# Graph attention on one core: half of M from scaled fp16 parts, joined probabilities, and a new order in the first rounds

## The reference

```python
h = relu((x - mean) / sqrt(var + 1e-05))
output = einsum('bni,io->bno', h, weight)
q, k = einsum('bni,io->bno', h, wq), einsum('bni,io->bno', h, wk)
alpha = einsum('bno,bmo->bnm', q, k)
alpha = maximum(alpha, 0.0) * (adj != 0)
alpha = softmax(alpha, axis=1)
return x + einsum('bnm,bmo->bno', alpha, output)
```

## Time and profile before

| | us |
|---|---|
| median of 3 runs | 412.75 (412.72 to 412.98) |
| the profiled execution | 412.91 |
| its span | 411.1 |
| TensorE busy | 405.3 (99%) |
| VectorE busy | 298.1 (73%) |
| ScalarE busy | 277.7 (68%) |
| GpSimd busy | 264.7 (64%) |

### The profile page before, as it was taken

One profiled execution on the slowest core, in us unless ns is written; L12 is line 12 of the kernel. 1 busy time (PEld: TensorE's weight loads), 2 busy tenths in 40 slices (PEclk: granted clock), 3 DMA queues, 4 the chain that ended last, 5 costly groups with the idle time before them and its releaser, 6 DMA issues.

```text
span 411.1 us, 9529 instructions
## 1 busy us (share of the span) xinstructions
PE 405.3 (99%) x3580; PEld 321.7 (78%) x3580; DVE 298.1 (73%) x571; ACT 277.7 (68%) x592; POOL 264.7 (64%) x286
## 2 busy tenths in 40 slices
PE   8999999999999999999999999999999999999995
PEld 5444545979797997979798897979889797979884
DVE  5797789896867676776767777676777667656565
ACT  4749887765867677766777776776867777644534
POOL 0767896979495866759395775939577584910004
PEclk9999999999999999999999999999999999999999
DMA  8973858989889897997969498985978599493022
GB/s 284 373 110 67 217 103 217 232 205 217 181 208 191 245 155 212 189 204 188 192 212 196 156 214 199 197 218 173 198 241 158 156 220 181 75 197 112 2 104 102
DMA packets 161641, 75.03 MB, mean 183 GB/s; under 512 B 135360, under 2 KB 143808, under 8 KB 161600
## 3 DMA queue, kind: packets, MB, share of 16 engines
q1 hardware_dynamic: 161168, 73.81, 77.6%
q10 hardware_dynamic: 432, 0.66, 0.4%
HBM read 24.12 MB, written 16.78 MB: 99 GB/s over the span
## 4 chain that ended last, share of the span: by engine, by line
PE 90%; DVE 4%; DMA 2%; ACT 1%; SPq 1%; issue 1%; POOL 0%; DVEq 0%; POOLq 0%
PE bank L1166 10%; PE bank L1165 10%; PE bank L1163 10%; PE bank L1181 10%; PE bank L1180 10%; PE bank L1178 10%; PE s_bank L1192 3%; PE s_bank L1193 3%; PE s_bank L1194 3%; PE bank L1199 2%; PE bank L1200 2%; PE bank L1201 2%; PE bank L1320 2%; PE bank L1322 2%; PE bank L1321 2%; DMA x_sb<-in_x 2%
## 5 line engine op out<-in xcount | busy, mean ns | idle before, releaser
L423 POOL TENSOR_TENSOR hn_lo<-h,hn_hi 128x512 f16<-128x512 f32 x64 | 74.0, 1166 | 53.1 <-ACT hn_hi L554 52.9
L544 ACT ACTIVATE h<-x_sb,shift,rstd 128x512 f32<-128x512 f32 x64 | 50.0, 804 | 24.0 <-POOL shift L418 23.6
L449 POOL TENSOR_TENSOR hn_lo<-s,hn_hi 128x512 f16<-128x512 f32 x56 | 63.3, 1163 | 0.3 <-ACT hn_hi L559 0.3
L1163 PE MATMUL bank<-hT_hi,mt_hi 128*128 128x256 f16 x224 | 61.1, 273 | 0.0
L1165 PE MATMUL bank<-hT_lo,mt_hi 128*128 128x256 f16 x224 | 61.1, 273 | 0.0
L1180 PE MATMUL bank<-wt_lo,hT_hi 128*128 128x256 f16 x224 | 61.1, 273 | 0.0
L1166 PE MATMUL bank<-hT_hi,mt_lo 128*128 128x256 f16 x224 | 61.1, 273 | 0.0
L1178 PE MATMUL bank<-wt_hi,hT_hi 128*128 128x256 f16 x224 | 61.1, 273 | 0.0
L1181 PE MATMUL bank<-wt_hi,hT_lo 128*128 128x256 f16 x224 | 61.1, 273 | 0.0
L559 ACT ACTIVATE hn_hi<-s 128x512 f16<-128x512 f32 x56 | 33.8, 625 | 25.6 <-POOL s L438 19.9
L1180 PE MATMUL bank<-w_lo,hT_hi 128*128 128x256 f16 x168 | 45.8, 273 | 0.0
(11 more groups left out here) (169 smaller groups left out, 1115.2 us busy)
## 6 DMA issues: line engine op xcount, KB each, us to landing
out_h<-x_sb SPq DMA_DIRECT2D x63, 256.0 KB, 2.1
x_sb<-in_x SPq DMA_DIRECT2D x15, 1024.0 KB, 5.5
adj_sb<-in_adj SPq DMA_DIRECT2D x16, 256.0 KB, 5.3
hn_hi<-in_L_gnn_wq SPq DMA_DIRECT2D x4, 256.0 KB, 5.6
x_sb<-in_x SPq DMA_DIRECT2D x2, 512.0 KB, 7.2
w_sb<-in_L_gnn_weight SPq DMA_DIRECT2D x2, 512.0 KB, 8.7
hn_lo<-in_L_gnn_wk ACTq DMA_DIRECT2D x2, 256.0 KB, 3.8
hn_lo<-in_L_gnn_wk SPq DMA_DIRECT2D x2, 256.0 KB, 3.7
```

Source lines behind the costliest of these rows:

```text
L423: nc.gpsimd.tensor_tensor(hn_lo[:, s, b], h[:, b], hn_hi[:, s, b], ALU.subtract).then_inc(h_split, 1)
L449: nc.gpsimd.tensor_tensor(low, s32[:, f], high, ALU.subtract).then_inc(s_split, 1)
L544: nc.scalar.activation(h[:, b], x_sb[:, s, b], ACT.Relu, bias=shift[:, b:b + 1], scale=rstd[:, b:b + 1]).then_inc(h_made, 1)
L1163: nc.tensor.matmul(o, bh[:, k, cols], ah[:, :, k], start=first and c == 0 and k == 0, stop=False, skip_group_check=True)
```

## The change

- **M.** Chunks 2 and 3 (`PARTS`) are made of fp16 parts. ScalarE makes high parts of wk and of two rows of wq, and a scaled copy of three quarters of wk. GpSimd makes three low parts of wk, VectorE the fourth and the low parts of wq. TensorE makes 24 products of 512 columns in place of 8 exact ones.
- **Scales.** wk, wq and W have a chain each (`top`, `top_row`, `power`; `spread_top`, `spread_row` on TensorE).
- **First V.** Its products go part by part, with a semaphore for each transpose.
- **Probabilities.** VectorE scales the exponentials in place, 128x512 at once; ScalarE makes the high part in one activation, VectorE the low part in one operation.
- **SP, round 1.** The transpose of the lows of group 2's sums moves behind the stores of group 0 and the load of x of group 4.
- **GpSimd.** The scales of group 3 come ahead of the last low of group 2's sums, those of group 4 behind the first low of group 3's.
- **VectorE and ScalarE, rounds 0 to 2.** A new order: in round 2 the mask of group 3 and the fourth `mt_lo` come behind the residuals, ahead of `sum_c22_t`; the exponentials and high parts of group 0 come two activations earlier.

```diff
@@ SP @@
+            def transpose_sums_hi(g):
                 sp.wait_ge(s_hi_made, sums(g, 4))
                 transpose_part(hT_hi, hn_hi, g % 2, GB, sT_landed)
+            def transpose_sums_lo(g):
                 sp.wait_ge(s_split, sums(g, 4))
                 transpose_part(hT_lo, hn_lo, g % 2, GB, sT_landed)
...
                     transpose_h(g + 1)
-                    transpose_sums(g + 1)
+                    transpose_sums_hi(g + 1)
+                    if g > 1:
+                        transpose_sums_lo(g + 1)
                 store(g - 1)
                 if g + 3 < G:
                     sp.wait_ge(stored[(g - 1) % UNROLL], 16 * GB * ((g - 1) // UNROLL + 1))
                     load_x(g + 3)
+                if g == 1:
+                    transpose_sums_lo(2)
                 if g + 1 < G:
                     transpose_mask(g + 1)
@@ GpSimd @@
-            lows_of_sums(2, 0)
-            layernorm_scales(3)
+            lows_of_sums(2, 0, scales=3, scales_at=3)
             sums_of_h(3, 1)
-            lows_of_sums(3, 1)
+            lows_of_sums(3, 1, scales=FIRST + 2, scales_at=1)
@@ ScalarE @@
+            act.wait_ge(scale_step, KEY_SCALED)
+            act.wait_ge(wkT_copied, K)
+            for k in range(K):
+                if k < 3:
+                    nc.scalar.activation(wk_scaled[:, k], wkT[:, k].rearrange("p r n -> p (r n)"), ACT.Copy,
+                                         scale=key_scale).then_inc(wk_scaled_made, 1)
+                nc.scalar.activation(wk_hi[:, k], wkT[:, k].rearrange("p r n -> p (r n)"), ACT.Copy,
+                                     scale=key_scale).then_inc(wk_hi_made, 1)
...
-                for b in graphs:
-                    nc.scalar.activation(p_hi[:, b], exps[:, b], ACT.Copy, scale=row_inv[:, b:b + 1]).then_inc(p_hi_made, 1)
+                nc.scalar.activation(p_hi[:], exps[:], ACT.Copy).then_inc(p_hi_made, GB)
@@ VectorE @@
+            def probabilities(g):
+                vec.wait_ge(inv_made, g + 1)
+                nc.vector.tensor_tensor(exps[:], exps[:], row_inv[:].unsqueeze(2).to_broadcast([N, GB, N]),
+                                        ALU.mult).then_inc(p_made, 1)
             def lo_of_p(g):
-                for b in range(GB):
-                    vec.wait_ge(p_hi_made, GB * g + b + 1)
-                    nc.vector.scalar_tensor_tensor(p_lo[:, b], exps[:, b], row_inv[:, b:b + 1], p_hi[:, b], ALU.mult,
-                                                   ALU.subtract).then_inc(p_split, 1)
+                vec.wait_ge(p_hi_made, GB * g + GB)
+                nc.vector.tensor_tensor(p_lo[:], exps[:], p_hi[:], ALU.subtract).then_inc(p_split, GB)
...
                 for b in range(1, GB):
                     residual(g - 1, (j - 1) % UNROLL, b)
+                if isinstance(g, int) and g == FIRST:
+                    lo_of_mt(3)
+                    make_mask(3, 1, 2)
+                    vec.wait_ge(mt_split, 4)
                 sum_c22_t(g)
...
+            vec.wait_ge(w_maxed, K)
+            top(KEY)
+            query_max(0)
+            top_row(KEY, 0)
+            query_max(1)
+            power(KEY, 0, 0)
+            query_max(2)
+            query_max(3)
+            vec.wait_ge(w_maxed, 2 * K)
+            top(QUERY)
+            stats_first(0)
+            stats_first(1)
+            top_row(QUERY, 1)
+            power(QUERY, 1, KEY_SCALED)
+            stats_first(2)
+            stats_first(3)
@@ TensorE @@
-            product_m(2, range(1))
-            pe.wait_ge(top_step, 3)
-            pe.wait_ge(consts_made, 5)
-            nc.tensor.matmul(top_bank[:, N:N + 3], ones[:], top_diag[:], start=True, stop=True).then_inc(top_filled, 1)
-            product_m(2, range(1, K))
-            product_m(3)
+            pe.wait_ge(wk_hi_made, K)
+            for c in PARTS:
+                pe.wait_ge(wq_hi_made, c - PARTS[0] + 1)
+                for k in range(K):
+                    scaled_m(c, wq_hi, wk_hi, k, start=k == 0)
+            spread_top(W, 2)
+            pe.wait_ge(wk_lo_pool, 3)
+            for c in PARTS:
+                for k in range(3):
+                    scaled_m(c, wq_hi, wk_lo, k)
+            spread_row(W, 2)
+            for c in PARTS:
+                pe.wait_ge(wq_lo_made, c - PARTS[0] + 1)
+                for k in range(K):
+                    scaled_m(c, wq_lo, wk_hi, k)
+            pe.wait_ge(wk_lo_vec, 1)
+            for c in PARTS:
+                scaled_m(c, wq_hi, wk_lo, 3, stop=True)
```

More of the change, by code:

```diff
@@ L157, in graph_attention_kernel @@
         shift = sb("shift", [N, GB], F32)
+        W, QUERY, KEY = range(3)
+        w_scale, key_scale, query_scale = (scale_of[:, i:i + 1] for i in (W, KEY, QUERY))
+        m_factor = W_TOP / (4 * D)
+        M_BACK = m_factor / 2.0 ** (2 * W_SHIFT)
         row_max = sb("row_max", [N, GB], F32)
@@ L253, in graph_attention_kernel @@
         s_split = sem("s_split")
-        hT0_landed = [sem(f"hT0_landed{b}") for b in range(3)]
+        hT0_hi_landed = [sem(f"hT0_hi_landed{b}") for b in range(3)]
+        hT0_lo_landed = [sem(f"hT0_lo_landed{b}") for b in range(3)]
         hT_landed = [sem(f"hT_landed{s}") for s in range(2)]
@@ L1006, in _, with top @@
             nc.vector.memset(alpha[:, 0:2], 0.0).then_inc(alpha_zeroed, 1)
[L1007 to L1014 removed]
+            def top(i):
+                nc.vector.tensor_reduce(w_top[:, i:i + 1], w_max[:, i], AX.X, ALU.max).then_inc(top_step, 1)
@@ L1031, in _ @@
-            vec.wait_ge(scale_step, 2)
-            nc.vector.tensor_scalar(w_scale[:].bitcast(I32), pow2[:, 0:1].bitcast(I32), -1.0, INV_BITS + W_SHIFT * 2.0 ** 23,
-                                    ALU.mult, ALU.add).then_inc(scale_step, 1)
+            top(W)
+            lo_of_wq(PARTS[0])
+            top_row(W, 2)
+            for r in PARTS[1:]:
+                lo_of_wq(r)
+            power(W, 2, M_SCALED + 1)
+            lo_of_wk(3)
             for k in range(K):
                 vec.wait_ge(w_hi_made, k + 1)
-                nc.vector.scalar_tensor_tensor(w_lo[:, k], w_sb[:, k], w_scale[:], w_hi[:, k], ALU.mult,
+                nc.vector.scalar_tensor_tensor(w_lo[:, k], w_sb[:, k], w_scale, w_hi[:, k], ALU.mult,
@@ L1053, in _ @@
+            stats_all(1, 1, 0)
+            stats_all(1, 1, 1)
             for k in range(K):
                 vec.wait_ge(m_hi_made, k + 1)
-                nc.vector.scalar_tensor_tensor(m_lo[:, k], M_BANK[k], m_scale[:], m_hi[:, k], ALU.mult,
+                nc.vector.scalar_tensor_tensor(m_lo[:, k], M_BANK[k], m_scale[:] if k not in PARTS else M_BACK, m_hi[:, k], ALU.mult,
                                                ALU.subtract).then_inc(m_split, 1)
+            stats_all(1, 1, 2)
+            stats_all(1, 1, 3)
@@ L1074, in _ @@
             softmax_sum(0)
+            probabilities(0)
             lo_of_p(0)
@@ L1103, in _ @@
             softmax_sum(LAST - 1)
+            probabilities(LAST - 1)
             lo_of_p(LAST - 1)
@@ L1303, in product_m, with spread_top, spread_row, scaled_m @@
                     last.then_inc(m_filled, 1)
+            def spread_top(i, n):
+                pe.wait_ge(top_step, 2 * n + 1)
+                nc.tensor.transpose(top_bank[0:1, 0:N], w_top[:, i:i + 1], ident[:]).then_inc(top_filled, 1)
+            def spread_row(i, n):
+                pe.wait_ge(top_step, 2 * n + 2)
+                pe.wait_ge(consts_made, 5)
+                nc.tensor.matmul(top_bank[:, N:N + 1], ones[:], top_col[:, i:i + 1], start=True, stop=True).then_inc(top_filled, 1)
+            def scaled_m(c, left, right, k, start=False, stop=False):
+                mm = nc.tensor.matmul(M_BANK[c], left[:, c - 2, k], right[:, k], start=start, stop=stop)
+                if stop:
+                    mm.then_inc(m_filled, 1)
+            def first_v(b, left, right, k, start=False, stop=False):
+                mm = nc.tensor.matmul(v_bank(0)[b], left[:, 0, b, k], right[:, k], start=start, stop=stop)
+                if stop:
+                    mm.then_inc(whole_v, 1)
             def whole_product_v(g, b):
@@ new lines, in _ @@
+            pe.wait_ge(wk_lo_vec, 1)
+            for c in PARTS:
+                scaled_m(c, wq_hi, wk_lo, 3, stop=True)
+            pe.wait_ge(hT0_hi_landed[0], 16)
+            for k in range(K):
+                pe.wait_ge(w_hi_made, k + 1)
+                first_v(0, hT_hi, w_hi, k, start=k == 0)
+            pe.wait_ge(hT0_lo_landed[0], 16)
+            for k in range(K):
+                first_v(0, hT_lo, w_hi, k)
+            pe.wait_ge(hT0_hi_landed[1], 16)
+            for k in range(K):
+                first_v(1, hT_hi, w_hi, k, start=k == 0)
@@ new lines, in _ @@
+            for k in range(K):
+                pe.wait_ge(w_split, k + 1)
+                first_v(0, hT_hi, w_lo, k, stop=k == K - 1)
+            for k in range(K):
+                first_v(1, hT_hi, w_lo, k)
+            pe.wait_ge(hT0_lo_landed[1], 16)
+            for k in range(K):
```

(9 more changed lines are left out.)

325 lines of the change are left out of this document (192 added, 133 removed).

## The result

The changed kernel takes 413.43 us (median of 21 runs, 413.0 to 414.32), the kernel before 412.73 in the same series (412.58 to 413.67, 21 runs). The ratio is 1.0016, 95% interval 1.0010 to 1.0023: 0.7 us slower, within the 0.2% that the prediction called no change, and resolved from zero only because there are so many runs. The profiled execution took 413.73, its span 411.9, 0.8 more than before.

The account below looks back on a forecast made before the run. TensorE, busy throughout from 97.10 to 380.00, was taken as the bound, so only time before 97.10 counted. Terms -0.8 - 0.2 + 0.8 + 0.2 = 0.0 against 412.91 gave 412.9; 8-in-10 range 411.6 to 414.1, with 0.1 above.

Parts of the forecast that it names:

- both terms of round 2: Round 2: TensorE's wait for the lows behind x, +0.8, and its wait for sum_c22_t on VectorE, +0.2.
- The start: Up to t's first product: fewer products for M let t start at 30.9 instead of 31.73, -0.8.
- rival B: Start gives nothing: m_scale and s_unscale at 1.24 each beside GpSimd delay W's top; 414.1, slower; chance 0.12.
- The outputs of group 0: Joined probabilities and earlier ScalarE activations close TensorE's 0.19 hole ahead of these outputs, -0.2.
- The lows behind x: Round 2: lows' transposes queued behind x of group 4 are ready at 74.7, wanted by TensorE at 73.9, +0.8.
- Rival A: Both round 2 waits stay away, the lows landing 0.6 behind x like the mask; 411.9, down to 411.6; chance 0.22.
- The landing beside the end of x: Alternative reading of the skill's section: lows counted as landed at 72.8, making their round 2 term 0.
- mt_lo and the mask: Round 2 on VectorE: both stand behind the residuals, ahead of sum_c22_t, ready 90.6 against TensorE's arrival at 90.4, +0.2.
- Nothing from round 3 on: Rounds from 3 on and the tail: no hole on TensorE, no term.
- What costs nothing: Joined probabilities from round 3 on, GpSimd's reordered scales, earlier x loads and ScalarE's ten activations for M: no cost.
- Rival C: Lows come late: x issued 3.85 after the last residual, a wait of 2.0 rather than 0.8; 413.9 left; chance 0.13.

Follow-up runs that it names:

- the early spreading: Changed kernel with TensorE spreading W's maximum after three of M's six low products: median 413.34, in two groups of runs; with the lows ahead of x too, 411.81.
- the kernels without the first hole: Changed kernel with the lows' transposes ahead of the load of x of group 4: 412.46; with W's maximum also spread earlier: 411.81.

## Why the prediction held, point by point

The forecast was no change, and the measured change is within its 0.2%. The waits came where they were put, but both terms of round 2 were too small.

- **The start**, -0.8 forecast, -0.8 measured (30.92 for 31.73). V starts 0.98 earlier (22.67 for 23.65), 0.96 forecast for TensorE's shorter list. The agreement of t's start to a tenth is in part luck: the same list gives 30.41 to 31.21 in six profiled executions, and the list of before 31.73 and, with SP's move alone, 31.27. The idle time in V is where it was put: 0.47 for w_hi's fourth part, 0.45 forecast. W's maximum took the way forecast to TensorE: the transposing product at 18.70 (18.8 forecast), w_hi at 21.18 (21.2). Two steps were off. The terms that the prediction lists for VectorE up to W's top add up to 18.3 and not to 18.8; it ended at 18.36, so VectorE did not hold TensorE at all, and the 0.2 of idle time there did not come. And m_scale and s_unscale took 0.24 and 0.15, 0.6 together forecast; rival B's 1.24 each did not come, and GpSimd was then busy with operations of 0.2 and 0.7. TensorE's own order behind that, the spreading product at 20.19 with its input there since 19.3, was what bound. The prediction did not see that it could be moved, which is worth 0.65 once the lows are ahead of x. No run has the start's change alone; that an earlier start reaches the end is shown by the early spreading.
- **The outputs of group 0**, -0.2 and -0.2.
- **The lows behind x**, +0.8 forecast, +1.3 measured. The order of events is as forecast, and so is the distance of the lows behind x, 1.9. The term is short by two small sizes, the issue of x (67.4 forecast, 67.61 measured) and its landing (5.4 and 5.6), so the lows were ready at 75.1 and not 74.7; the last 0.1 is rounding and the step from the landing to the product. Rival A, by which 16 blocks land 0.6 behind as the mask did, is refuted: 1.9 here, 1.9 with the early spreading, and 3.2 in the kernel before with SP's move. The Trainium skill, "DMA: Bandwidth & Descriptors", section "Queues, rings and completion order", has the increment land behind that engine's earlier writes. The run with the early spreading agrees: lows that were issued at 67.0 were not counted as landed before x was at 74.7. The landing beside the end of x, which the prediction read out of the section as a term of 0, did not come.
- **mt_lo and the mask**, +0.2 forecast, +0.5 measured. The pair's price was right, 2.2 us for 1.2 + 1.07, with mt_lo at 0.99 and the mask at 1.38. The residuals ended at 88.5, 87.6 forecast, and TensorE arrived at 90.86, 90.4 forecast. 0.5 of both is the first hole, which was larger by that. The other 0.4 of the residuals is a step that failed: the forecast took their end from VectorE's own work, and they wait for the outputs, whose first product starts at 84.34; VectorE stood idle for 1.41 ahead of them.
- **Nothing from round 3 on**: right for the changed kernel, no hole from 98 to 380. But in the kernels without the first hole the residual of round 3 comes 0.36 to 0.59 late for the fourth output. "What costs nothing" was true behind a hole, not in itself.
- **Rival C** did not come: x was issued 2.8 after the last residual (64.84 to 67.61), 2.7 forecast, and not 3.85.

The sum of the forecast was 0.0, the profiles give +0.8, the medians +0.7: both terms of round 2 were too small, by 0.5 and 0.3, and none had the wrong sign. The total stayed inside the 0.2% (0.8 us) only just, with both misses on the same side.

## What to carry to other kernels

A transfer that the next product needs does not belong behind a large load in the same queue: here it cost 1.3 us, 2.6 in the kernel before, and made the time hang on the end of the load, which in one profile came 2.5 us late; behind the small stores and ahead of the load the hole was gone. A repair is worth less than its hole, 0.97 of 1.30 here, since the next chain is close behind, and two repairs need not add. Where one engine is busy throughout, a microsecond saved at the start is real only if every later wait moves with it: look for the first product in each round whose operand comes by another clock. And an operation on VectorE that can be held by GpSimd should be costed by both of its prices, since a shift of some tenths swaps one for the other.

## What was not expected of the hardware

- A hole of 2.58 us on TensorE was followed by 3.4 us at a granted clock of 0.5, for 1.6 us more. Four of that kernel's six runs have the lower mean clock (0.996), two have 1.000. In the execution with the 3.2 us hole (early spreading alone) the clock stayed at 1.00, so it is not each such hole.
- The load of x of group 4, 1 MB, landed after 5.4 to 6.3 us in the profiled executions, and after 8.1 in one, by its DMA share with one DMA engine behind.
- The same mt_lo took 0.68 to 1.60 us, the same mask 0.41 to 1.49, by where GpSimd's 128x512 operations stood. The Trainium skill, "SBUF — State Buffer", section "Who interferes with whom", has the two engines share a port pair that one of them locks for a whole instruction. The lengths fit that; no run here isolates it.
- SP's issue of a 16-block transpose took 4.9 to 7.5 us right behind the load of x, 2.9 to 3.0 right behind the stores, and 1.7 to 2.1 for the three that stand ahead of the stores.
